# Query and key projections through a full-height staging tile, with DMAs spreading the halves

## What is computed

```python
def xattn(q, kv, Wq, Wk, Wv, Wo, bo):          # q (8,512,256), kv (8,512,128)
    qh, kh, vh = heads(q @ Wq), heads(kv @ Wk), heads(kv @ Wv)      # 16 heads of 64
    scores = einsum('bhnd,bhmd->bhnm', qh, kh) * 64 ** -0.5
    out = einsum('bhnm,bhmd->bhnd', softmax(scores), vh)
    return merge(out) @ Wo + bo

def ffn(x, gate_w, expert_w, expert_b):
    probs = softmax(x @ gate_w.T)
    comb = top2_weights(probs)                  # (tokens, 8), zero but for two
    return sum(comb[:, e] * (x @ expert_w[e].T + expert_b[e]) for e in range(8))

x = x + tanh(g_xattn) * xattn(layernorm(x), ctx, Wq, Wk, Wv, Wo, bo)
x = x + tanh(g_ffn) * ffn(layernorm(x), gate_w, expert_w, expert_b)
```

## Time and profile before

| what | us |
|---|---|
| median of 3 runs | 1217.59 (1215.83 to 1218.45) |
| the profiled execution, whole | 1210.17 |
| its span, first to last instruction | 1208.5 |

### The profile page before, as it was taken

The page is one execution under the profiler, slowest core; times in us unless marked ns, Lnnn a source line. Parts: engine busy times, 40 slices in busy tenths (PEclk is TensorE's granted clock), DMA queues, the critical chain, the costliest instruction groups (busy, mean ns, idle before and its releaser), DMA issues.

```text
span 1208.5 us, 30873 instructions
## 1 busy us (share of the span) xinstructions
PE 1135.7 (94%) x10592; PEld 913.4 (76%) x10592; DVE 979.0 (81%) x1945; ACT 849.6 (70%) x1531; POOL 648.0 (54%) x579
## 2 busy tenths in 40 slices
PE   4888999999999999999899999999999999999968
PEld 3677777788778887788777887778877788778846
DVE  7788878987898778987789877898778887897646
ACT  4888888676876678676786768867687677866610
POOL 2566666455655547455564545645556455654610
PEclk8999999999999999999999999999999999999979
DMA  4333212122221122221222112211122121121000
GB/s 133 78 85 79 37 37 54 29 37 45 37 53 29 28 54 36 46 37 27 57 37 45 28 37 45 54 36 28 41 50 45 28 37 40 33 37 36 2 19 17
DMA packets 97521, 51.79 MB, mean 43 GB/s; under 512 B 77000, under 2 KB 86608, under 8 KB 97360
## 3 DMA queue, kind: packets, MB, share of 16 engines
q1 hardware_dynamic: 97360, 49.74, 20.3%
HBM read 11.68 MB, written 4.19 MB: 13 GB/s over the span
## 4 chain that ended last, share of the span: by engine, by line
PE 70%; DVE 15%; issue 7%; DMA 3%; ACT 3%; SPq 1%; DVEq 0%; POOL 0%; ACTq 0%
PE MB L934 30%; PE PV L1057 12%; PE MX L1037 8%; PE ST L1047 7%; PE ST L1044 7%; DVE nmax L767 3%; DVE KA L744 3%; PE MB L944 3%; DMA QB<-nmax 2%; DVE QB L739 1%; PE MB L1014 1%; DVE stats L656 1%; DVE w L879 1%; SPq L432 1%; DVE m L886 1%
## 5 line engine op out<-in xcount | busy, mean ns | idle before, releaser
L514 POOL TENSOR_TENSOR p_s<-pf,p_s 128x512 f16<-128x512 f32 x512 | 594.7, 1169 | 496.1 <-ACT p_s L621 492.5
L596 ACT ACTIVATE pf<-ST 128x512 f32<-128x512 f32 x512 | 306.2, 599 | 193.0 <-PE ST L1047 186.3
L767 DVE TENSOR_REDUCE nmax<-MX 128x1 fp32r<-128x512 f32 x512 | 347.2, 685 | 69.0 <-PE MX L1037 60.9
L621 ACT ACTIVATE p_s<-pf 128x512 f16<-128x512 f32 x512 | 318.1, 629 | 45.1 <-PE PV L1057 42.0
L1037 PE MATMUL MX<-KA,QA 128*128 128x512 f32 x512 | 216.9, 426 | 18.6 <-DVE nmax L767 15.2
L1057 PEld LDWEIGHTS PV<-v_s,p_s 128*128 128x128 f16 x6144 | 193.6, 98 | 33.6 <-issue 24.7
L1047 PE MATMUL ST<-QB,KB 65*128 65x512 f32 x512 | 204.8, 400 | 7.2 <-DMA QB<-nmax 7.0
L1057 PE MATMUL PV<-v_s,p_s 128*128 128x65 f16 x6144 | 209.0, 194 | 1.3 <-POOL p_s L514 1.3
L1044 PE MATMUL ST<-QA,KA 128*128 128x512 f32 x512 | 206.2, 403 | 3.6 <-ACT pf L596 3.1
L934 PE MATMUL MB<-ex_s,x2t_s 128*128 128x512 f32 x708 | 188.8, 402 | 3.2 <-DVE KA L744 3.2
L934 PEld LDWEIGHTS MB<-ex_s,x2t_s 128*128 128x128 f32 x708 | 128.1, 188 | 34.9 <-DVE KA L744 6.3
(11 more groups left out here) (120 smaller groups left out, 1113.4 us busy)
## 6 DMA issues: line engine op xcount, KB each, us to landing
QA<-QA SPq DMA_DIRECT2D x64, 256.0 KB, 3.0
KB<-KA SPq DMA_DIRECT2D x64, 256.0 KB, 3.0
QB<-nmax SPq DMA_DIRECT2D x512, 0.5 KB, 1.9
xin<-x SPq DMA_DIRECT2D x8, 512.0 KB, 4.0
out<-acc SPq DMA_DIRECT2D x8, 512.0 KB, 3.2
kvin<-kv_t SPq DMA_DIRECT2D x8, 256.0 KB, 4.2
acc<-expert_t SPq DMA_DIRECT2D x8, 256.0 KB, 3.3
acc<-wo SPq DMA_DIRECT2D x4, 256.0 KB, 3.3
```

The costliest lines, as they stand in the source:

```text
L514: pool.tensor_tensor(p_s[:, h % 2, 1, t, :], pf[:, t, :], p_s[:, h % 2, 0, t, :], ALU.subtract)\
L596: act.activation(pf[:, t, :], st_bank(h, t)[:, :], ACT.Exp, bias=P_SHIFT, scale=SCALE)\
L621: act.activation(p_s[:, h % 2, 0, t, :], pf[:, t, :], ACT.Copy).then_inc(p_hi, 1)
L767: dve.tensor_reduce(nmax[:, h % 2, t:t + 1], MX[t % 2][:, :], AX.X, ALU.max, negate=True)\
```

## The change

Outside the prologue, a pair's q or k projection is taken whole: one activation of 128 rows writes its high part into a staging tile (q_hl or k_hl, [128, 2, 512]), one tensor_tensor of 128 rows its low part beside it. DMAs of 64 rows by 512 (128 KB) bring the parts to their places: four for q into QA, two and two for k into KA (copy_first), and later two into KB and two into QB (copy_second): 12 DMAs for a pair where 2 stood. KB and QB hold two pairs instead of three. copy_second is issued at the start of each even head, in front of its rows; the q copies are issued two slots after the projection's slot, the k copies three slots after. ACT and DVE wait, before they overwrite the staging tile, for the copies of the pair before; the first maximum of a pair waits for its KA copies instead of DVE's low part. The table places k 2 in (0, 3) instead of (1, 1), k 3 in (2, 3) instead of (3, 0), k 4 and k 5 in the slots of q 4 and q 5, (4, 2) and (6, 1), instead of (5, 0) and (7, 0), and moves v 2, wo 3 and q 3 one or two slots up.

```diff
@@ -63,14 +63,14 @@
 PLACED = {
-    (0, 0): [("v", 0, 0)], (0, 1): [("v", 1, 0)], (0, 2): [("q", 2)], (0, 3): [("v", 2, 0)],
-    (1, 0): [("v", 3, 0)], (1, 1): [("k", 2)], (1, 2): [("ot", 7)],
-    (2, 1): [("wo", 3, 0)], (2, 2): [("wo", 3, 1)], (2, 3): [("q", 3)],
-    (3, 0): [("k", 3)], (3, 1): [("v", 0, 1)], (3, 2): [("ot", 0)], (3, 3): [("v", 1, 1)],
+    (0, 0): [("v", 0, 0)], (0, 1): [("v", 1, 0), ("v", 2, 0)], (0, 2): [("q", 2)], (0, 3): [("k", 2)],
+    (1, 0): [("v", 3, 0)], (1, 2): [("ot", 7)],
+    (2, 0): [("wo", 3, 0)], (2, 1): [("wo", 3, 1)], (2, 2): [("q", 3)], (2, 3): [("k", 3)],
+    (3, 1): [("v", 0, 1)], (3, 2): [("ot", 0)], (3, 3): [("v", 1, 1)],
...
+        def qa_count(it, p):
+            return 64 * it.copied(p) + 16
...
+            def copy_first(it, name):
 
                 kind, p = name
                 s = it.pair_slot(name)
...
+                for i in range(2):
+                    rows = slice(HEAD * i, HEAD * (i + 1))
+                    if kind == "q":
+                        sp.dma_start(QA[0:HEAD, s + i, :].bitcast(F32), q_hl[rows, 0, :].bitcast(F32))\
+                          .then_inc(qa_in[p % 2], 16)
+                        sp.dma_start(QA[HEAD:P, s + i, :].bitcast(F32), q_hl[rows, 0, :].bitcast(F32))\
+                          .then_inc(qa_in[p % 2], 16)
+                    else:
+                        sp.dma_start(KA[0:HEAD, s + i, :].bitcast(F32), k_hl[rows, 0, :].bitcast(F32))\
+                          .then_inc(ka_in[p % 2], 16)
+                if kind == "k":
+                    sp.wait_ge(job_free, it.done(JOBS, name) + BANKS)
+                    for i in range(2):
+                        rows = slice(HEAD * i, HEAD * (i + 1))
+                        sp.dma_start(KA[HEAD:P, s + i, :].bitcast(F32), k_hl[rows, 1, :].bitcast(F32))\
+                          .then_inc(ka_in[p % 2], 16)
+
+            def copy_second(it, h):
+
+                p = h // 2 + 1
+                sp.wait_ge(st_ready, tile_count(it.b, h - 1, TT - 1))
+                for i in range(2):
+                    rows = slice(HEAD * i, HEAD * (i + 1))
+                    sp.dma_start(KB[0:HEAD, 2 * (p % 2) + i, :].bitcast(F32), k_hl[rows, 0, :].bitcast(F32))\
+                      .then_inc(kb_in[p % 2], 16)
+                    sp.dma_start(QB[0:HEAD, 2 * (p % 2) + i, :].bitcast(F32), q_hl[rows, 1, :].bitcast(F32))\
+                      .then_inc(qb_in[p % 2], 16)
...
+                    if h % 2 == 0 and t == 0 and not (it.kind == FIRST and h == 0) and \
+                            not (it.kind == LAST and h == HEADS - 2):
+                        copy_second(it, h)
                     if maximum_at(it.kind, h, t):
                         row(it, *maximum_at(it.kind, h, t))
-                    for name in taken_in(it.kind, h, t):
-                        if name[0] in "qk":
-                            copy(it, name)
+                    for kind, later in (("q", 1), ("k", 2)):
+                        n = h * TT + t - later
+                        for name in taken_in(it.kind, n // TT, n % TT) if n >= 0 else []:
+                            if name[0] == kind:
+                                copy_first(it, name)
...
+                    last = act.activation((q_hl if kind == "q" else k_hl)[:, 0, :], m[:, :], ACT.Copy)
...
+                    last = dve.tensor_tensor(hl[:, 1, :], m[:, :], hl[:, 0, :].bitcast(F32), ALU.subtract)
...
+                                following = h // 2 + 1
+                                if early_pair(it, following):
+                                    pe.wait_ge(job_free, it.start(JOBS) + BANKS)
+                                else:
+                                    pe.wait_ge(ka_in[following % 2], ka_count(it, following))
+                                pe.wait_ge(qa_in[following % 2], qa_count(it, following))
```

More of the change, by code:

```diff
@@ L368, in head_count, with ka_count, qb_count, kb_count @@
             return b * HEADS + (h + 1)
-        def dup_count(b, p):
-            return 16 * (b * (PAIRS // 2) + (p // 2 + 1))
+        def qa_count(it, p):
+            return 64 * it.copied(p) + 16
+        def ka_count(it, p):
+            return 64 * it.copied(p)
+        def qb_count(it, p):
+            return 32 * it.copied(p)
+        def kb_count(it, p):
+            return 32 * it.copied(p) + 16
+        def early_pair(it, p):
+            return it.kind == FIRST and p < 2
         late = [(wo[256 * k:256 * (k + 1), :].rearrange("(c p) n -> p c n", p=P),
@@ L417, in _, with copy_early @@
             sp.dma_start(gt_f[:, :, :], gate_t.rearrange("(c p) e -> p c e", p=P)).then_inc(small_in, 16)
-            def copy(it, name):
+            def copy_early(it, name):
+                kind, p = name
+                heads = slice(2 * p, 2 * p + 2)
+                dst, src, copied = ((QA[HEAD:P, heads, :], QA[0:HEAD, heads, :], qa_in) if kind == "q" else
+                                    (KB[0:HEAD, heads, :], KA[0:HEAD, heads, :], kb_in))
+                sp.wait_ge(job_hi, it.done(HI, name))
+                sp.dma_start(dst.bitcast(F32), src.bitcast(F32)).then_inc(copied[p % 2], 16)
@@ L440, in _ @@
                         row(pro, 0, t)
-                copy(pro, name)
+                copy_early(pro, name)
             for t in range(TT // 2):
@@ L549, in take_hi @@
                 kind = name[0]
-                if kind in ("q", "k"):
+                if kind in ("q", "k") and it.kind != PRO:
+                    p = name[1]
+                    if name == ("q", 2):
+                        act.wait_ge(job_free, it.start(JOBS) + BANKS)
+                    elif kind == "q":
+                        act.wait_ge(job_free, it.done(JOBS, ("q", (p - 1) % PAIRS)) + BANKS)
+                    before = p - 1 if p >= 2 else p - 1 + PAIRS
+                    if not early_pair(it, before):
+                        if kind == "q":
+                            act.wait_ge(qa_in[before % 2], qa_count(it, before))
+                        else:
+                            act.wait_ge(ka_in[before % 2], ka_count(it, before))
+                            act.wait_ge(kb_in[before % 2], kb_count(it, before))
+                    last = act.activation((q_hl if kind == "q" else k_hl)[:, 0, :], m[:, :], ACT.Copy)
+                elif kind in ("q", "k"):
                     dst, s = (QA if kind == "q" else KA), it.pair_slot(name)
@@ L735, in take @@
                 dve.wait_ge(job_hi, it.done(HI, name))
-                if kind == "q":
+                if kind in ("q", "k") and it.kind != PRO:
+                    p = name[1]
+                    before = p - 1 if p >= 2 else p - 1 + PAIRS
+                    hl = q_hl if kind == "q" else k_hl
+                    if not early_pair(it, before):
+                        if kind == "q":
+                            dve.wait_ge(qb_in[before % 2], qb_count(it, before))
+                        else:
+                            dve.wait_ge(ka_in[before % 2], ka_count(it, before))
+                    last = dve.tensor_tensor(hl[:, 1, :], m[:, :], hl[:, 0, :].bitcast(F32), ALU.subtract)
+                elif kind == "q":
                     s = it.pair_slot(name)
@@ L1083, in slot @@
                 b, kind = it.b, it.kind
[L1084 removed]
+                p = h // 2
                 if h % 2 == 0 and t == 0:
[L1086 removed]
+                    pe.wait_ge(kb_in[p % 2], kb_count(it, p))
+                    if not early_pair(it, p):
+                        pe.wait_ge(qb_in[p % 2], qb_count(it, p))
                 for part in PE_ORDER[h % 2][t].split():
```

32 lines of the change are left out of this document (15 added, 17 removed), and 6 rows, old and new, of the table PLACED.

## The result

The change makes the kernel slower. Median 1271.5 us (1266.37 to 1275.79, 4 runs) against 1218.02 (1215.83 to 1219.28, 4 runs) of the kernel before beside it: a ratio of 1.0439, 95% interval 1.0397 to 1.0482. The prediction was 1210, range 1183 to 1235: wrong, in size and in direction. The profiled execution after is 1266.37 us with a span of 1264.6, against 1210.17 and 1208.5.

What follows compares the result with a forecast made beforehand. PE was taken as the bound, with about 10 us a batch of waiting. Relief of 5.3 us less 4.4 for copies gave -0.9 us a batch, -7 in eight batches: from 1217.59 to about 1210 us, range 1183 to 1235.

Steps and rivals of the forecast that it cites:

- What bounds the kernel: PE's matmuls fill 133 to 134 of 143.7 us a batch; about 10 us is waiting, all in heads 0 to 9.
- The relief of 5.3 us a batch: Spared DVE and ACT steps ahead of PE's waits: 1.1 us in heads 1 and 2, 1.7 in 3, 2.5 in 7 to 9.
- Head 3: Fewer projection steps ahead of the maximum of slot (3, 2): worth 1.7 us a batch to PE, between 0 and 2.
- heads 7 to 9: k 5's steps leave head 7, q 6 and k 6 lose one each: 2.5 us a batch, between 0 and 2.8.
- Moved jobs: nothing: The table's moved jobs cost nothing: same matmuls, and DVE had freed the needed bank a slot before in every case checked.
- my four places: Batch turn, head 2's first score, head 4's slot 2, head 6's first score: copies cost 4.4 us a batch together.
- The turn of the batch: Row of slot (0, 1) goes behind output, context and four copies, at about 444.7: cost 0.9 us, between 0 and 1.4.
- slot (4, 2): Head 4: PE's first maximum on pair 3 waits for KA copies: cost 2.0 us a batch, between 0.7 and 3.0.
- Head 2's first score: q 2's low part waits for QB copies, and slot (1, 1)'s row stands behind four copies: cost 1.2 us, 0 to 2.
- Slot (6, 2): ACT's exponential queued behind k 5's wait for a KB copy: costed at nothing, up to 2 us if the cover fails.
- The first batch at the same price: The first batch, with no output at its turn but later DVE waits, was given the same -0.9 us as the others.
- the bursts are slow: Rival, chance 0.28: copies in a burst land after 3.7 us instead of 3.0, giving 1233, or 1249 with ACT stopped too.

Runs made afterwards that it cites:

- e3: Kernel before, with ACT and DVE leaving out the steps for each pair's second head in all batches but the first, no DMAs added: ratio 0.990.
- e1: Kernel before with the new table of placed jobs and nothing else: ratio 1.031.
- e5: Changed kernel, but the four copies at an even head's start read a weight tile, so ACT and DVE need not wait for them: ratio 1.027.
- e8: Changed kernel with the table's heads 4 to 7 as before the change, k 4 in (5, 0) and k 5 in (7, 0): ratio 1.055.
- e13: Changed kernel, but the load of the next batch's x (512 KB) is issued at the end of head 6 instead of head 5: ratio 1.048.

## Why the prediction was wrong

**What bounds the kernel** was right: about 11 us of waiting in most LOOP batches, none to be had in heads 10 to 15, which kept their time. The starts were the better guide than the busy share of the weight loads. All DVE and ACT steps that the change spares, in seven of the eight batches, brought 11 us (e3), and the weight loads' share fell from 76 to 73% while the kernel got slower. The Trainium skill (Perfetto Trace Analysis, Identifying the Most-Contended Engine) names that share, beside the FLOPs done against the peak, as the measure of how near TensorE is to its limit; my estimate of 1130 us by it is not borne out.

**The relief of 5.3 us a batch** was mis-sized: e3 shows about 2 (in the median LOOP batch 11.5 to 9.2). Head 3 gave 1.4 of the 1.7, heads 1 and 2 0.9 of 1.1. Then head 4 takes back 1.0: PE comes earlier and waits for nmax there. And heads 7 to 9 gave 0.7 of 2.5; heads 8 and 9 did not move at all (9.9 and 9.0 us long in both). "DVE sets the pace" had been read from a busy share, 27.86 of 30.24 us, the very thing I had warned of for PE. What counts is whether PE waits for it, and in heads 8 and 9 it hardly does.

**Moved jobs: nothing** is the step that failed most: 37 us by itself (e1). In the changed kernel it does not come to 37, as head 3 shows, but it is one of the two causes in the dearest place, slot (6, 3): the new table makes the wo job there the one that needs the bank of q 5, and DVE's step that frees it now waits for copies. I asked only whether a bank is free when PE's third next job comes. I did not ask what stands behind the moved steps on DVE: k 3's steps passed the layer norm and o_n, and PE's transpose waited 2.60 us. And I took the bank of q 5 as free because DVE had freed banks a slot earlier in the old trace, though I had just put a wait in front of DVE's step.

**The copies.** Landing 3.0, between 1.9 and 3.5: the median was 2.4, better than I took. But at the turn, one of my four places, it was 3.9 to 4.2, with output and context directly ahead, and in slot (6, 2), which I had priced apart, 4.5 to 4.6, with x ahead. Of k 3's KA copies the last took 3.4, and why is open. I had the row for it (3.45 us behind two large transfers), and used it as an end of the range rather than as the value for the places behind large transfers. The turn of the batch was the right place, taken at 0.9 and worth 2.0 in head 1, as the row goes 5.7 us after the output where I had 4.2. In slot (4, 2) the wait on the KA copies came, at 4.0 us in all instead of 16; but heads 3 and 4 together, which I had at +0.3 us a batch, came to +0.8, since head 3 gave 0.7 and not 1.7. Head 2's first score cost nothing that can be seen.

**Slot (6, 2)** was the right neighbourhood and the wrong engine. I followed ACT behind the KB copy and priced it at nothing; PE was held by DVE behind the QB copy issued with it, and head 6 waits 4.1 us a batch longer. DVE's waits of this kind are 44.7 us in all:

```profile
DVE q_hl L817 <- DMA QB<-q_hl: 44.7, 31, 3.1
```

and PE behind DVE, with the clock's fall on top. The cover I named (a slot and a half) was for the exponential, not for what else stands on the staging tile.

**The first batch at the same price** failed: 22.7 us more instead of 0.9 less. e1 puts 11.6 of that on the table, e5 some 6.6 on the staging waits, each to within the 3.5 us that this batch varies by. There the late weights stand in SP's order as well. In e1 the row for head 6 made PE wait 3.10 us, and the next 6 us are at half clock, of which the first 2 stand here:

```profile
83.40:86.40 3.00, 0.00 (x0) 0.00 (x0) 1.29 (x2) 1.15 (x3) 1.19 (x2) 0.92 0.47 111
86.40:88.40 2.00, 1.99 (x19) 1.47 (x20) 0.73 (x2) 1.81 (x4) 0.00 (x0) 0.50 0.63 172
```

How the remaining 4 to 5 us divide between rows behind copies and the clock was not separated.

The rival "the bursts are slow", at 0.28, had the sign. Its landing of 3.7 us was passed at the turn (3.9 to 4.2) but not in head 4 (3.4) nor by the copies of q (2.4), and it had no term for the table. Even with its worst case, 1249, it lay 22 us short.

## What to carry to other kernels

When a step moves up in an engine's order, list what it now stands in front of, not only whether its own inputs and outputs are ready; and where a change adds a wait, price everything queued behind the waiting step, and every buffer that step frees. A DMA's price is that of its place in the queue: behind 512 KB it is not the median's. Time spared on an engine counts only where another engine's waits name it, and even then the next wait takes part of it back. Where an instruction waits for several things, work out from the kernel when each was ready before believing the name: in e8 the profile named DVE, and the copies were the cause.

## What the runs showed of the hardware

A wait of PE can cost more than itself. Behind 2.31 us idle in head 6 the granted clock was 0.50 for the next 2.75 us, and behind 3.10 us in e1's first batch for 6. Behind the 1.75 us at the turn it stayed at 1.00, and so it did behind e1's 2.60 in head 3, though e13's 2.60 at head 8 was followed by 0.79 and 0.50. So the length of the wait alone doesn't decide it, and what does was not tried.

A small copy landed later where a large one was issued just ahead: in the batch shown, 128 KB within the core took 2.3 us with its kind ahead of it, 3.9 to 4.2 behind 512 + 256 KB and 4.5 to 4.6 behind 512 KB, and a row of 512 bytes took 1.9, and 3.3 behind the copies at the turn. For the 512 KB, e13 shows it by moving them: 2.3. An issue took SP about 0.60 us at each of such copies, and 1.53 us at the first row behind four of them (479.19).
